# Cross-attention block: normalisation of x moved from VectorE to GpSimd, and the output's sum put in front of a block transpose

## The reference

```python
def _ln(x, g, b):
    mu = jnp.mean(x, axis=-1, keepdims=True)
    var = jnp.mean(jnp.square(x - mu), axis=-1, keepdims=True)
    return (x - mu) * jax.lax.rsqrt(var + EPS) * g + b
def _attn(x, ctx, Wq, Wk, Wv, Wo, bo):          # 16 heads of 64
    sim = jnp.einsum('bihd,bjhd->bhij', q, k) * scale
    attn = jax.nn.softmax(sim, axis=-1)
    out = jnp.einsum('bhij,bjhd->bihd', attn, v).reshape(b, n, INNER)
    return out @ Wo + bo
h = _ln(x, g1, be1)
x = _attn(h, h, Wq1, Wk1, Wv1, Wo1, bo1) + x
h = _ln(x, g2, be2)
x = _attn(h, context, Wq2, Wk2, Wv2, Wo2, bo2) + x
```

## Time and profile before

| what | value |
|---|---|
| median of 3 runs | 3169.32 us (3163.63 to 3170.73) |
| the profiled execution's own time | 3167.35 us |
| its span | 3165.5 us |
| PE busy | 2988.4 us, 94% of the span |
| DVE, ACT, POOL busy | 75%, 59%, 40% |
| mean granted TensorE clock | 0.991 of full speed |

### The profile page before, as it was taken

One profiled execution on the slowest core, in us unless ns is written; L12 is line 12 of the kernel. 1 busy time (PEld: TensorE's weight loads), 2 busy tenths in 40 slices (PEclk: granted clock), 3 DMA queues, 4 the chain that ended last, 5 costly groups with the idle time before them and its releaser, 6 DMA issues. The chain is left out here.

```text
span 3165.5 us, 77555 instructions
## 1 busy us (share of the span) xinstructions
PE 2988.4 (94%) x25600; PEld 2601.8 (82%) x25600; DVE 2364.2 (75%) x4043; ACT 1856.1 (59%) x5615; POOL 1265.0 (40%) x783
## 2 busy tenths in 40 slices
PE   7999999999999998799999999999999969999999
PEld 6888888888888887688888888888888848888888
DVE  6777877777777776788888888888888856555654
ACT  6666666666666665566666666666666632233232
POOL 4444444444444444444444444444444420001100
PEclk9999999999999999899999999999999989999999
DMA  8887878788788887588778878878887850000100
GB/s 248 240 237 235 240 234 240 237 242 240 236 240 239 240 238 235 177 237 237 237 239 237 237 235 242 239 234 244 239 237 237 234 146 27 27 27 33 33 27 20
DMA packets 464422, 624.99 MB, mean 197 GB/s; under 512 B 57728, under 2 KB 397056, under 8 KB 464128
## 3 DMA queue, kind: packets, MB, share of 16 engines
q1 hardware_dynamic: 460256, 624.09, 66.3%
q10 hardware_dynamic: 4128, 0.41, 0.1%
HBM read 330.71 MB, written 293.60 MB: 197 GB/s over the span
## 5 line engine op out<-in xcount | busy, mean ns | idle before, releaser
L367 POOL TENSOR_TENSOR cross_probs<-cross_probs,cross_row_inv 128x1024 f32<-128x1024 f32 x256 | 484.7, 1893 | 652.2 <-DVE cross_row_inv L570 652.2
L367 POOL TENSOR_TENSOR self_probs<-self_probs,self_row_inv 128x1024 f32<-128x1024 f32 x256 | 484.8, 1894 | 642.7 <-DVE self_row_inv L570 642.7
L412 ACT ACTIVATE cross_probs<-cross_ps_s,cross_neg_max 128x256 f32<-128x256 f32 x1024 | 473.3, 472 | 139.3 <-DVE cross_blocks L562 69.1
L412 ACT ACTIVATE self_probs<-self_ps_s,self_neg_max 128x256 f32<-128x256 f32 x1024 | 472.9, 473 | 79.0 <-DVE self_neg_max L543 51.7
L543 DVE TENSOR_REDUCE self_neg_max<-self_ps_s 128x2 f32<-128x512 f32 x512 | 328.2, 682 | 141.7 <-PE self_ps_s L716 141.7
L543 DVE TENSOR_REDUCE cross_neg_max<-cross_ps_s 128x2 f32<-128x512 f32 x512 | 331.0, 683 | 113.0 <-PE cross_ps_s L716 112.1
L562 DVE STREAM_TRANSPOSE cross_blocks<-cross_probs 128x1024 f32<-128x1024 f32 x256 | 318.2, 1243 | 119.3 <-POOL cross_probs L367 108.1
L562 DVE STREAM_TRANSPOSE self_blocks<-self_probs 128x1024 f32<-128x1024 f32 x256 | 317.9, 1242 | 111.8 <-POOL self_probs L367 104.6
L464 ACT ACTIVATE self_qk_hi<-self_ps_qk 128x512 fp32r<-128x512 f32 x256 | 153.2, 598 | 233.0 <-PE self_ps_s L716 153.3
L464 ACT ACTIVATE cross_qk_hi<-cross_ps_qk 128x512 fp32r<-128x512 f32 x256 | 152.7, 596 | 209.0 <-PE cross_ps_s L716 151.4
L976 ACT ACTIVATE ff_u_hi<-ff_gated 128x512 fp32r<-128x512 f32 x128 | 80.9, 632 | 301.5 <-PE ff_ps_y L1116 214.2
(11 more groups left out here) (166 smaller groups left out, 9579.6 us busy)
## 6 DMA issues: line engine op xcount, KB each, us to landing
self_turns<-self_blocks SPq DMA_DIRECT2D x1024, 128.0 KB, 2.8
self_probs_t<-self_turns SPq DMA_DIRECT2D x256, 512.0 KB, 4.4
cross_turns<-cross_blocks SPq DMA_DIRECT2D x1024, 128.0 KB, 2.8
cross_probs_t<-cross_turns SPq DMA_DIRECT2D x256, 512.0 KB, 4.4
self_xt<-in_x SPq DMA_DIRECT2D x32, 256.0 KB, 6.3
self_xres<-in_x SPq DMA_DIRECT2D x32, 256.0 KB, 2.7
after_self_attention<-yout SPq DMA_DIRECT2D x32, 256.0 KB, 2.4
cross_xt<-after_self_attention SPq DMA_DIRECT2D x32, 256.0 KB, 6.2
```

Source lines behind the costliest of these rows:

```text
L367: pool.tensor_tensor(tile, tile, scale, ALU.mult).then_inc(probs_ready, 1)
L412: last = act.activation(probs[:, slot % 2, h, t], scores[:, slot % 2, h, t], ACT.Exp, bias=neg_max[:, slot % 2, i:i + 1], accum_out=row_su ...
```

## The change

Three things change in `attention`; the feed-forward stage keeps its code. DVE no longer adds epsilon and no longer writes `xnorm`. POOL does both, in step 2, behind its two `normalise`: epsilon is added from a new constant tile `eps`, the power follows, then x minus the mean and the product with `rstd`, each as one instruction over both token tiles with a broadcast operand. And DVE makes the output's sum in front of the younger pair's `turn` instead of behind its `inverse`.

```diff
@@ pool
             def norm_power(b):
-                pool.wait_ge(var_ready, b + 1)
+                pool.wait_ge(meanvar_ready, TT * (b + 1))
                 if counts(c := b):
                     pool.wait_ge(xnorm_ready, c)
+                pool.tensor_tensor(var_eps[:], meanvar[:, :, 1], eps[:], ALU.add).then_inc(var_ready, 1)
+                pool.wait_ge(var_ready, b + 1)
                 pool.tensor_tensor(rstd[:], var_eps[:], minus_half[:], ALU.pow).then_inc(rstd_ready, 1)
+
+            def norm_apply(b):
+                pool.wait_ge(rstd_ready, b + 1)
+                if counts(c := b):
+                    pool.wait_ge(h_transposed, c)
+                mean = meanvar[:, :, 0:1].to_broadcast([P, TT, DIM])
+                pool.tensor_tensor(xnorm[:], xt[:], mean, ALU.subtract).then_inc(centred, 1)
+                pool.wait_ge(centred, b + 1)
+                pool.tensor_tensor(xnorm[:], xnorm[:], rstd[:].unsqueeze(2).to_broadcast([P, TT, DIM]),
+                                   ALU.mult).then_inc(xnorm_ready, 1)
...
                 if part in (FIRST, LOOP) and p == 2:
                     norm_power(b + 1)
+                    norm_apply(b + 1)
@@ vector
-                dve.wait_ge(meanvar_ready, TT * (b + 1))
-                nc.vector.tensor_scalar(var_eps[:], meanvar[:, :, 1], EPS, None, ALU.add).then_inc(var_ready, 1)
-
-            def norm_apply(b):
-                dve.wait_ge(rstd_ready, b + 1)
-                if counts(c := b):
-                    dve.wait_ge(h_transposed, c)
-                for t in range(TT):
-                    last = nc.vector.tensor_scalar(xnorm[:, t], xt[:, t], meanvar[:, t, 0:1], rstd[:, t:t + 1],
-                                                   ALU.subtract, ALU.mult)
-                last.then_inc(xnorm_ready, 1)
...
                 if part != DRAIN:
                     low_parts(g, p)
+                if part != FIRST and p == 6:
+                    output(b - 1)
                 if alive(part, p + 1, TURNED):
                     turn(b, p + 1)
                 if alive(part, p + 1, NORMED):
                     inverse(b, p + 1)
                 if part in (FIRST, LOOP) and p == 2:
                     norm_stats(b + 1)
-                if part != FIRST and p == 6:
-                    output(b - 1)
```

More of the change, by code:

```diff
@@ L170, in attention @@
         minus_half = sb("minus_half", [P, TT], F32)
+        eps = sb("eps", [P, TT], F32)
         xt = sb("xt", [P, TT, DIM], F32)
@@ L226, in attention @@
         rstd_ready = sem("rstd_ready")
+        centred = sem("centred")
         xnorm_ready = sem("xnorm_ready")
@@ L335, in _ @@
             pool.memset(minus_half[:], -0.5).then_inc(half_made, 1)
-            pool.wait_ge(half_made, 1)
+            pool.memset(eps[:], EPS).then_inc(half_made, 1)
+            pool.wait_ge(half_made, 2)
             def norm_power(b):
-                pool.wait_ge(var_ready, b + 1)
+                pool.wait_ge(meanvar_ready, TT * (b + 1))
                 if counts(c := b):
                     pool.wait_ge(xnorm_ready, c)
+                pool.tensor_tensor(var_eps[:], meanvar[:, :, 1], eps[:], ALU.add).then_inc(var_ready, 1)
+                pool.wait_ge(var_ready, b + 1)
                 pool.tensor_tensor(rstd[:], var_eps[:], minus_half[:], ALU.pow).then_inc(rstd_ready, 1)
+            def norm_apply(b):
[7 more added lines that the diff above has]
+                                   ALU.mult).then_inc(xnorm_ready, 1)
             def low_h(b):
@@ L382, in _ @@
             norm_power(0)
+            norm_apply(0)
             low_h(0)
@@ L609, in step @@
                         maxima(g + 1 - SCORES, (p + 1 - SCORES) % 2, h)
-                if part in (FIRST, LOOP) and p == 2:
-                    norm_apply(b + 1)
             norm_stats(0)
-            norm_apply(0)
             if cross:
```

## The result

| what | before | changed |
|---|---|---|
| median | 3168.8 us (3163.63 to 3170.73, 5 runs) | 3185.97 us (3182.96 to 3192.19, 5 runs) |
| ratio to before | | 1.0051, 95% interval 1.0039 to 1.0062 |
| the profiled execution: time, span | 3167.35, 3165.5 us | 3187.82, 3186.0 us |
| PE busy | 2988.4 us | 3001.8 us |
| DVE, POOL busy, share of the span | 75%, 40% | 71%, 44% |

The kernel is 0.5% slower: 17.2 us by the medians, 20.5 us by the spans of the two profiled executions. The clock is nearly the same and PE runs the same 25600 matmuls, so what was added is waits. That PE busy grew by 13.4 us all the same has its cause in how the profile counts: 0.25 us of each wait of PE stands in its busy rows and not in the list (worked out under part 1), and PE has 214 waits where it had 156. As an estimate, 58 x 0.25 = 14.5 us.

The account below looks back on a forecast made before the run. PE, busy 94%, was taken as the bound, then DVE's path to `o_lo`, then SP's queue at the seam. Terms -36 + 53 + 3 + 1 = +21 us gave 3189 us, own range 3175 to 3205, wider range 3162 to 3212.

Parts of the forecast that it names:

- part 1: Normalisation leaves DVE: step 4's `o_lo` comes earlier, gaining 0.42 us per sequence in self, 0.78 in cross, 36 us in all.
- steps 0 and 2 lose (parts 2, 3): At the seam between sequences: 53 us lost through the later transpose and SP's queue, 3 us through DVE's context part.
- outside the loops: At the start of each stage POOL's normalisation chain is exposed, about 0.5 us each time, 1 us in all.
- the cancelling rival: Gain and loss cancel because 0.5 to 0.7 us of the shift gets through: 3163 to 3175 us; chance 13%.
- Part 2: Sum before younger transpose delays it 1.22 us (self), 0.96 (cross); through SP's queue 0.93 and 0.83 per sequence, 53 us lost.
- the "about 0.4 us" of the forecast: Sign in step 4 of cross: a PE wait for `o_lo` of about 0.4 us remains in the profile after.
- The wait of step 2: Sign in cross: PE waits for `o_lo` behind DVE's wait for `turns<-blocks`, the latter over 1 us on average.
- The new wait for `probs_t` in step 0 of self: Sign: PE newly waits about 1 us for `probs_t` in step 0 of self.
- Part 3: Cross: PE's 0.6 us wait for POOL's low context part is covered in step 0; DVE's context part costs 3 us.
- The shift was not absorbed: Rival at the seam: transfers catch up, less than 0.6 us of the shift gets through, 3137 us; chance 16%.
- POOL does not hold the transpose: Rival: DVE's step 4 transpose or cross's copy waits 0.6 to 1.2 us for POOL's new instructions, 3220 us; chance 8%.
- POOL is not late: Rival: POOL's new instructions exceed 1.3 us each, delaying its next `normalise` a few tenths per sequence, 3200 us; chance 4%.

Follow-up runs that it names:

- k3_after_store_first: The changed kernel, with SP issuing the output store before the younger pair's four block stores; 3114.15 us, ratio 0.9813 to the kernel before.
- k7_sum_between: The changed kernel, with the output's sum between the younger pair's transpose and its reciprocal; 3124.54 us, ratio 0.9858 to the kernel before.
- k1_norm_only: The changed kernel with the output's sum back behind the younger transpose, so only the normalisation moves to POOL; 3124.55 us, ratio 0.9844 to the kernel before.
- k2_sum_only: The kernel before with only the output's sum moved in front of the younger transpose; 3232.94 us, ratio 1.0192.
- k4_norm_store_first: The kernel before with POOL normalising x and the output store issued before the younger pair's block stores, sum behind the transpose; 3108.12 us, ratio 0.9801.

## Why the prediction was right, point by point

The forecast was 3189 us and the median is 3185.97, inside the forecast's own range of 3175 to 3205. By the medians the change cost 17.2 us where 20 were forecast. The terms, in us per sequence and then for 30 sequences:

| term | predicted: self, cross | measured: self, cross | total |
|---|---|---|---|
| step 4 gains (part 1) | 0.42, 0.78 | 0.68, 0.78 | -36 predicted, -43.8 measured |
| steps 0 and 2 lose (parts 2, 3) | 0.93, 0.93 | 1.00, 1.00 | +56, +60.0 |
| outside the loops (measured: the remainder) | | | +1, +4.3 |
| sum | | | +21, +20.5 |

That the sum agrees to within 1 us is luck in part. The three terms were off by 7.8, 4.0 and 3.3 us, and the first error was taken back by the other two. Three slips of the working stand beside it. 3188 us and 2 us more are 3190, not 3189. And the bounds of 33 and 65 us for the loss give 3170 to 3202, not 3175 to 3205; the measured time lies in both. And where 0.5 to 0.7 us of the shift gets through, the working gives 3167 to 3179 us, not the 3163 to 3175 of the cancelling rival.

**Part 1.** The mechanism held, and POOL's side with it. The timeline of POOL and DVE between steps 2 and 4 of the changed kernel:

```profile
609.19 1.89 POOL L382 TENSOR_TENSOR self_probs<-self_probs,self_row_inv 128x1024 f32<-128x1024 f32 x1 [1.42 <-DVE self_row_inv L576]
611.04 0.19 POOL L345 TENSOR_TENSOR self_var_eps<-self_meanvar,self_eps 128x2 f32<-128x2 f32 x1
611.31 0.71 POOL L347 TENSOR_TENSOR self_rstd<-self_var_eps,self_minus_half 128x2 f32<-128x2 f32 x1
612.10 1.04 POOL L354 TENSOR_TENSOR self_xnorm<-self_xt,self_meanvar 128x512 f32<-128x512 f32 x1
613.22 1.04 POOL L356 TENSOR_TENSOR self_xnorm<-self_xnorm,self_rstd 128x512 f32<-128x512 f32 x1
613.55 1.24 DVE L568 STREAM_TRANSPOSE self_blocks<-self_probs 128x1024 f32<-128x1024 f32 x1
...
614.93 1.89 POOL L382 TENSOR_TENSOR self_probs<-self_probs,self_row_inv 128x1024 f32<-128x1024 f32 x1 [0.67 <-DVE self_row_inv L576]
```

1.04 us each lies between the bounds of 0.95 and 1.27, POOL is done at 614.26, 3.2 us after its `normalise` (3.2 to 3.9 predicted), and still idles 0.67 us before the next. The split worked out ahead, 0.28 and 0.14 us for epsilon and 0.64 for `xnorm`, was measured as 0.33, 0.14 and 0.63 to 0.65. The one mis-sized term is what PE can use of it in self. The step said "Self can use only what PE waits: 0.38 us in the row, and not more than 21.1/35 = 0.60 us on average", and took 0.42. As a mean of the listed waits that was right: over the 29 sequences it is 0.44 us. But PE gained 0.68 us. The listed idle time is not all that a wait costs. In the kernel before, step 4 of self is 10.00 to 10.05 us long plus the listed wait, in every one of the 29 sequences, whether the wait is 0.27 or 0.56 us; without a wait it is 9.78 in the changed kernel. So 0.25 us of each wait is not in the list. The timeline of PE before, at the row with the wait and at the same place of step 6, which has none, shows where it is:

```profile
609.73 0.40 PE L669 MATMUL self_ps_misc<-self_hi_wv,self_h_lo 128*128 128x256 f32 x2
...
610.73 0.28 PE L749 MATMUL self_ps_y<-self_hi_wo,self_o_lo 128*128 128x256 f32 x1
...
620.16 0.40 PE L669 MATMUL self_ps_misc<-self_hi_wv,self_h_lo 128*128 128x256 f32 x2
620.40 0.28 PE L749 MATMUL self_ps_y<-self_hi_wo,self_o_hi 128*128 128x256 f32 x1
620.52 0.28 PE L749 MATMUL self_ps_y<-self_hi_wo,self_o_lo 128*128 128x256 f32 x1
```

With the wait the first `project_out` matmul starts 610.51 - 609.73 = 0.78 us after the row of L669, without it 0.24: 0.54 us are lost, and 0.38 are listed, because a matmul's row (0.28 us) is longer than the distance to the next (0.12), and the rest of the row hides the beginning of the wait. The next matmul follows after 0.22 us in place of 0.12, 0.10 more. Where a wait only shrinks, as in cross from 1.18 to 0.42 us, this part stays, and the list gives the gain (0.76 against 0.78); where it vanishes, the part comes back as well. The steps' lengths would have given the bound.

**Part 2.** The first link was exact: 1.22 and 0.96 us of delay were predicted for the younger transpose, and 1.21 and 0.94 us were measured. The chain through SP's queue was shown by `k3_after_store_first` and `k7_sum_between`. How much gets through was put at 0.93 in self and 0.83 in cross. It was 1.00 in self, out of a shift of the loads of 11.94 - 10.66 = 1.28 us, so 0.28 us was slack there. In cross the loads moved by 0.99 us and the steps lost 0.91 us against `k1_norm_only`, 0.95 us in `k2_sum_only` against before: almost no slack. The loss in cross also holds part 3. The step that was off by this much was "as about half of the passes wait, I take the chain to be on time on average". The table of the seam shows that the loads of before already stood at the edge.

The timeline of PE and DVE in cross of the changed kernel:

```profile
1879.73 0.38 PE L752 MATMUL cross_ps_y<-cross_hi_wo,cross_o_hi 128*128 128x256 f32 x1 [0.42 <-DVE cross_o_lo L581]
1891.44 1.24 DVE L568 STREAM_TRANSPOSE cross_blocks<-cross_probs 128x1024 f32<-128x1024 f32 x1
1895.20 1.02 DVE L542 TENSOR_TENSOR cross_c_hi<-cross_c_t,cross_c_hi 64x256 fp32r<-64x256 f32 x1
1896.87 0.39 PE L656 MATMUL cross_ps_qk<-cross_c_hi,cross_hi_wk 128*128 128x256 f32 x1 [0.37 <-POOL cross_c_lo L367]
1899.51 0.39 PE L752 MATMUL cross_ps_y<-cross_hi_wo,cross_o_hi 128*128 128x256 f32 x1 [0.63 <-DVE cross_o_lo L581]
1907.31 1.25 DVE L568 STREAM_TRANSPOSE cross_blocks<-cross_probs 128x1024 f32<-128x1024 f32 x1 [0.70 <-DMA cross_turns<-cross_blocks]
1909.24 0.39 PE L752 MATMUL cross_ps_y<-cross_hi_wo,cross_o_hi 128*128 128x256 f32 x1 [0.63 <-DVE cross_o_lo L581]
```

Step 4's wait of 0.42 us is the "about 0.4 us" of the forecast (1.18 before). The wait of step 2 at 1909.24, behind DVE's wait for its slot at 1907.31, is the one that was forecast. The new wait for `probs_t` in step 0 of self is 0.72 us on average over the 29 sequences, where about 1 us was forecast.

**Part 3.** The list has 0.37 us for the wait for the context's low part. From start to start it is the 0.6 us of the forecast: 1896.10 to 1896.87 is 0.77 us where the same two matmuls were 0.23 apart before (1878.50, 1878.73), and the next follows 0.10 us later than there. The later wait for `o_lo` shrinks from 1.19 to 0.63 us. Over the 29 sequences the two places cost +0.65 and -0.56 us, so the cover held here but for 0.09 us. It fails once the queue is mended. `k3_after_store_first` still has this wait (11.4 us in its list, 31 times), and its step 0 of cross takes 10.40 us where `k4_norm_store_first` takes 10.10. DVE's part of the context grew from a mean of 982 to 1054 ns, 2 us in all.

**The rivals.** The shift was not absorbed: of 1.28 us 1.00 came through in self, of 0.99 us 0.91 in cross, and the loss went in the kernels that moved the store or the transpose. POOL does not hold the transpose: 1.24 us at 613.55, more than half of it beside L356 (which ends at 614.26), against 1.23 before. Nor does the copy of the context in cross grow: its median is 0.68 us in both kernels, and in the changed one it runs beside L354 (1675.14 to 1675.82, L354 from 1675.16). POOL is not late.

## What to carry to other kernels

An in-order queue that holds a wait for a landing is a serial chain even when hardly any compute engine seems to wait for it. A listed wait of PE costs more than its idle time (0.25 us here), so what its removal is worth is read from the distance between starts. Before an instruction is placed in front of another, follow what the second one releases through such queues. A transfer that is ready early and has to be waited for should be issued first, so that what becomes ready later is issued while it is in flight: here the place of that one line was worth 72 us in the changed kernel, and 16 us where the sum stood behind the transpose (`k1_norm_only` against `k4_norm_store_first`). And a change of two parts should be timed in parts: this one hid a gain of 1.6% behind a loss of 1.9%.

## What the runs showed of the hardware

An addition of two elements on DVE took 1.04 us beside a POOL instruction, and on POOL the same work took 0.20 us. DVE's L542, with two inputs in SBUF, took 1.02 us at 1895.20, beside POOL's `h_lo` (1894.67 to 1895.94), where before its fastest took 0.42. The block transpose kept its 1.24 us beside POOL's L356. The Trainium skill ("SBUF — State Buffer", Who interferes with whom) says that a DVE instruction with two SBUF inputs contends with a GpSimd instruction that reads SBUF, and one with a single SBUF input outside the 2-port modes does not; the rows of L542 and of the transpose agree.

For a store of 256 KB to HBM it was 2.53 us from its issue to the next issue, behind the wait for its landing (631.10 to 633.63). The Trainium skill ("DMA: Bandwidth & Descriptors", Anatomy of one DMA) says that a DMA's fixed cost of about 2.0 us is mostly the wait for the last byte's receipt, and that semaphore waits are held by the issuing sequencer. The row agrees with the second point and is of the size of the first, but does not show how its 2.53 us divide. The four stores of 1.8 us in `k3_after_store_first`, issued between that store and the wait, show that the queue can issue other transfers while it is in flight. That section describes DMAs issued from GpSimd; these are issued from SP.
